# Half the norm matmuls moved to GpSimd adds, a mask in small tiles, ten value moves, full-array norm turns and new step orders in a one-core transformer kernel

## What is computed

```python
for i in range(DEPTH):                                    # 6 layers, 16 batches each
    x = attn_layer(shift_tokens(x), Wqkv[i], q_scale[i], k_scale[i], Wo[i]) + x
    x = ffn_layer(shift_tokens(x), ln_g[i], ln_b[i], W1[i], b1[i], W2[i], b2[i]) + x

def attn_layer(x, Wqkv, qs, ksc, Wo):
    q, k, v = heads of (x @ Wqkv)
    q, k = l2norm(q) * qs, l2norm(k) * ksc                # per head and token
    q, k = rotary(q) * scale, rotary(k) / scale
    sim = (q . k over this window and the one before) * 8, masked to 32 keys back, none before token 0
    return softmax(sim) @ v @ Wo
```

## Time and profile before

| what | value |
|---|---|
| median of 3 runs | 3445.39 us (3439.58 to 3446.2) |
| the profiled execution, its own time | 3448.65 us |
| its span from first to last instruction | 3446.9 us |
| mean granted clock of TensorE, share of full speed | 0.991 |
| busy share PE / ACT / DVE / POOL | 97% / 78% / 71% / 42% |
| DMA, mean | 122 GB/s |

### The profile page before, as it was taken

One profiled execution on the slowest core, in us unless ns is written; L12 is line 12 of the kernel. 1 busy time (PEld: TensorE's weight loads), 2 busy tenths in 40 slices (PEclk: granted clock), 3 DMA queues, 4 the chain that ended last, 5 costly groups with the idle time before them and its releaser, 6 DMA issues.

```text
span 3446.9 us, 152524 instructions
## 1 busy us (share of the span) xinstructions
PE 3333.7 (97%) x63228; PEld 2469.4 (72%) x63228; DVE 2439.3 (71%) x5141; ACT 2701.8 (78%) x9033; POOL 1445.0 (42%) x1276
## 2 busy tenths in 40 slices
PE   7789999999999999999999999999999999999997
PEld 4457777777777777777777777777777777777775
DVE  5667777777777777777777777777777767777773
ACT  5667887878787787878788787877878787887875
POOL 2244443444444354444444443453434444443441
PEclk9999999999999999999999999999999999999998
DMA  2056655665655666565565655565565656556563
GB/s 73 1 109 132 131 123 126 134 136 115 147 118 125 129 137 132 128 131 123 120 148 117 139 128 128 122 138 127 121 141 120 132 127 133 122 121 136 114 135 75
DMA packets 361274, 421.43 MB, mean 122 GB/s; under 512 B 52291, under 2 KB 265814, under 8 KB 359814
## 3 DMA queue, kind: packets, MB, share of 16 engines
q1 hardware_dynamic: 360582, 411.67, 55.2%
HBM read 19.30 MB, written 2.10 MB: 6 GB/s over the span
## 4 chain that ended last, share of the span: by engine, by line
PE 70%; POOL 18%; issue 4%; DVE 2%; ACT 1%; DMA 0%; SPq 0%; POOLq 0%; DVEq 0%
PE ring_ps L1234 16%; POOL qs L617 13%; PE out_ps L1326 12%; PE out_ps L1336 10%; PE ring_ps L1279 8%; PE small_ps L1245 6%; PE score_ps L1297 4%; PE ring_ps L1308 4%; PE ring_ps L1372 4%; POOL probs L601 3%; DVE prod L993 2%; PE ring_ps L1269 2%; PE out_ps L1350 2%; PE score_ps L1289 1%; PE small_ps L1253 1%
## 5 line engine op out<-in xcount | busy, mean ns | idle before, releaser
L774 ACT ACTIVATE probs<-score_ps,neg_max,rq 128x64 f32<-128x64 f32 x3072 | 1194.7, 420 | 95.7 <-DVE neg_max L1031 94.5
L993 DVE TENSOR_TENSOR prod<-ring_ps,tables 128x512 f32<-128x512 f32 x1536 | 956.9, 680 | 285.6 <-PE ring_ps L1234 257.8
L617 POOL TENSOR_TENSOR ks<-prod 128x1024 f32<-128x1024 f32 x192 | 452.7, 2358 | 852.5 <-DVE prod L993 852.4
L1234 PE MATMUL ring_ps<-xs,wqk 128*128 128x256 f32 x3072 | 768.9, 388 | 15.5 <-issue 10.6
L774 ACT ACTIVATION_READ_ACCUMULATOR probs<-score_ps,neg_max,rq 128x1 f32 x3072 | 677.1, 220 | 0.0
L730 ACT ACTIVATE square<-ring_ps,biases 128x512 f32<-128x512 f32 x768 | 516.9, 687 | 197.2 <-DVE prod L993 196.0
L1234 PEld LDWEIGHTS ring_ps<-xs,wqk 128*128 128x128 f32 x3072 | 571.1, 191 | 104.3 <-issue 17.6
L601 POOL TENSOR_TENSOR probs<-probs,inv_sums 128x512 f32<-128x512 f32 x384 | 401.1, 1045 | 576.0 <-DVE inv_sums L1045 576.0
L617 POOL TENSOR_TENSOR qs<-prod 128x1024 f32<-128x1024 f32 x192 | 453.4, 2361 | 395.4 <-DVE prod L993 395.4
L1326 PEld LDWEIGHTS out_ps<-pt,v 64*64 64x64 f32 x24576 | 397.0, 135 | 113.5 <-issue 111.6
L763 ACT ACTIVATE att_t<-out_ps 128x512 f32<-128x512 f32 x384 | 217.0, 591 | 297.3 <-PE out_ps L1326 297.2
(11 more groups left out here) (182 smaller groups left out, 3835.6 us busy)
## 6 DMA issues: line engine op xcount, KB each, us to landing
v<-vs SPq DMA_DIRECT2D x1344, 128.0 KB
qt<-qs SPq DMA_DIRECT2D x768, 128.0 KB
kt<-ks SPq DMA_DIRECT2D x768, 128.0 KB
v<-vs SPq DMA_DIRECT2D x192, 64.0 KB
wqk<-in_L_ffn_Wqkv SPq DMA_DIRECT2D x6, 1024.0 KB, 5.1
wv<-in_L_ffn_Wqkv SPq DMA_DIRECT2D x6, 512.0 KB, 5.8
wo<-in_L_ffn_Wo SPq DMA_DIRECT2D x6, 512.0 KB
out_dram<-ks SPq DMA_DIRECT2D x16, 128.0 KB, 1.9
```

The lines of the kernel that those rows point to most:

```text
L617: pool.tensor_tensor(dst, prod_a[p % 2], prod_b[p % 2], ALU.add).then_inc(rot_ready, 1)
L774: last = nc.scalar.activation(probs[i][:, j, e, :], score_ps[e][:, KEYS * j:KEYS * (j + 1)], ACT.Exp, bias=neg_max[:, h:h + 1], scale=rq[p ...
L993: last = V.tensor_tensor((prod_b if a else prod_a)[p % 2][:, f, :] .rearrange("p (u c) -> p u c", u=2), bank[:, :].rearrange("p (u c) -> p ...
L1234: last = mm(bank_of(s)[:, TOKENS * f:TOKENS * (f + 1)], wqk[:, n, 2 * c + f, a, :], xs[:, WINDOW:PADDED], start=True, stop=True)
```

## The change

It touches one mechanism in each of five places and writes all orders anew.

1. **Sums of squares.** A new POOL step AS adds `square[couple][1]` to `square[couple][0]`, once per couple (4 per batch-layer). NK and NQ then run 4 matmuls in place of 8 and wait for the adds instead of for the squares.
2. **Mask.** The two full-array matmuls per query tile become eight of 64 rows by 32 columns, each over 512 columns, in the tile shape of the scores. The constants shrink to one mask per 64 rows and a selector.
3. **Norm turns.** `rk_bf`, `rkt` and `head_sel_bf` are padded with zeros to 128, so TU and KN use the full array.
4. **Value moves.** 10 DMAs per batch-layer in place of 16, with the same bytes; six of them span 64 partitions.
5. **`pt`** gets a buffer for each query tile, so TC waits for the PV of the previous batch-layer and not for that of the previous tile.

```diff
-V_MOVES = 16
+V_MOVES = 10
 PE_ORDER = """
-PA0 PB0 PA1 S00 S01 PB1 BI WO PA2 NK CEN PB2 VAR PA3 PB3 TK UP0 UP1 S10 S11 V0 UP2 T00 TU NQ KN0 PAD V1 PV00 KN1
-TQ T01 V2 DN T10 PV01 V3 T11 PV10 PV11
+PA0 PB0 S00 S01 BI PAD PB1 PA1 WO PA2 NK PB2 CEN PB3 VAR PA3 TK S10 S11 UP0 UP1 T00 UP2 TU V1 KN0 PV00 KN1 NQ
+T01 V3 DN PV01 T10 TQ V0 V2 T11 PV10 PV11
 DVE_ORDER = """
-XS RA0 RB0 RA1 M0 RB1 BI XA XB AR00 RA2 RB2 CK XG RB3 RA3 H0 M1 AR01 H1 TC00 UC H2 KM0 CQ VC1 KM1 AR10 TC01 X
-AR11 TC10 VC3 TC11
+XS RA0 RB0 BI M0 RB1 RA1 XA RA2 XB AR00 RB2 CK RB3 RA3 XG M1 H0 TC00 AR01 UC H1 H2 KM0 VC1 KM1 AR10 TC01 CQ VC3
+X AR11 TC10 TC11
 ACT_ORDER = """
-QA0 QB0 QA1 E00 QB1 E01 E02 SQ QA2 LN E03 QB2 RTK LG G0 QB3 QA3 G1 VC0 G2 LE E10 E11 E12 E13 VC2 OC00 OC01 OC10
-RTQ OC11
+QA0 QB0 E00 QB1 QA1 E01 E02 QA2 SQ E03 LN RTK QB2 LG G0 QB3 QA3 G1 G2 LE E10 E11 E12 E13 OC00 OC01 RTQ VC0 VC2
+OC10 OC11
 POOL_ORDER = """
-AD0 AD1 AD2 AN00 AD3 RK TB0 AN01 TB1 AN10 TB2 AN11 TB3
+AD0 AS0 AS1 AD1 AN00 AD2 AD3 RK AS2 TB0 TB1 TB2 AN01 AS3 AN10 TB3 AN11
...
+                    top, low = KEYS * e, KEYS * e + WINDOW
+                    for m in range(WPT - 1):
+                        sp.dma_start(v2[top:top + KEYS, m + 1::WPT, :], vs[WINDOW * m:WINDOW * m + KEYS, :, e, :]
+                                     ).then_inc(v_moved, 16)
+                    sp.dma_start(v2[low:low + WINDOW, 0::WPT, :], vs[0:WINDOW, :, e, :]).then_inc(v_moved, 16)
+                    sp.dma_start(v2[top:top + WINDOW, WPT, :], vs[P - WINDOW:P, 0, e, :]).then_inc(v_moved, 16)
...
+                if kind == "AS":
+                    p = s[1]
+                    last_square = max(rank(ACT_ORDER, (x, p), "QA", "QB") for x in ("QA", "QB"))
+                    pool.wait_ge(sq_ready, at(g, QK_BANKS, last_square + 1))
+                    one, other = square[p % COUPLES]
+                    pool.tensor_tensor(one[:, :], one[:, :], other[:, :], ALU.add).then_inc(sq_summed, 1)
...
-                    dve.wait_ge(pv_ready, at(g, TILES, i))
-                    V.tensor_copy(pt[:, 4 * c:4 * c + 4, :], bank_of(("T", i, c))[:, :].rearrange("p (j c) -> p j c", c=P)
+                    if g > 0:
+                        dve.wait_ge(pv_ready, at(g - 1, TILES, i + 1))
+                    V.tensor_copy(pt[i][:, 4 * c:4 * c + 4, :], bank_of(("T", i, c))[:, :].rearrange("p (j c) -> p j c", c=P)
...
-                    pe.wait_ge(sq_ready, at(g, QK_BANKS, last_square + 1))
+                    pe.wait_ge(sq_summed, at(g, 2 * COUPLES, COUPLES * (n + 1)))
                     pe.wait_ge(norms_ready, at(g, 2, n))
-                    for a in range(2):
-                        for u in range(QUADS):
-                            last = mm(norm2_ps[WINDOW * u:WINDOW * (u + 1), :], head_ones[:, :],
-                                      square[u // 2][a][:, TOKENS * (u % 2):TOKENS * (u % 2 + 1)],
-                                      start=(a == 0), stop=(a == 1), skip_group_check=True)
+                    for u in range(QUADS):
+                        last = mm(norm2_ps[WINDOW * u:WINDOW * (u + 1), :], head_ones[:, :],
+                                  square[u // 2][0][:, TOKENS * (u % 2):TOKENS * (u % 2 + 1)],
+                                  start=True, stop=True, skip_group_check=True)
...
-                    turn = bank_of(s)[0:3 * HEADS, 0:TOKENS // 2].bitcast(BF16)
+                    turn = bank_of(s)[:, 0:TOKENS // 2].bitcast(BF16)
...
-                        for e in range(2):
-                            if e == 1 and i == 0:
-                                pe.wait_ge(q_moved, moved(g, 1))
-                            mm(score_ps[e][:, :], ident_bf[:, :], mask_bf[:, i, :, :].rearrange("p j c -> p (j c)"),
-                               start=True, stop=False, skip_group_check=True)
+                        for w in range(WPT):
+                            for e in range(2):
+                                if (w, e) == (WPT - 1, 1) and i == 0:
+                                    pe.wait_ge(q_moved, moved(g, 1))
+                                mm(score_ps[e][WINDOW * w:WINDOW * (w + 1), :],
+                                   mask_sel_bf[64 * e:64 * e + 64, int((i, w) == (0, 0)), :],
+                                   mask_bf[64 * e:64 * e + 64, :, :].rearrange("p j c -> p (j c)"),
+                                   start=True, stop=False, skip_group_check=True)
```

More of the change, by code:

```diff
@@ L32 @@
 MOVES = 8
-V_MOVES = 16
+RK_PARTS = P // HEADS
+V_MOVES = 10
 V_STEPS = 2 * TILES
@@ L138, in build @@
         ident_bf = sb("ident_bf", [P, P], BF16)
-        mask_bf = sb("mask_bf", [P, TILES, PAIRS, KEYS], BF16)
+        mask_bf = sb("mask_bf", [P, PAIRS, KEYS], BF16)
+        mask_sel_bf = sb("mask_sel_bf", [P, 2, WINDOW], BF16)
         head_ones = sb("head_ones", [P, WINDOW])
-        head_sel_bf = sb("head_sel_bf", [3 * HEADS, QUADS, P], BF16)
+        head_sel_bf = sb("head_sel_bf", [P, QUADS, P], BF16)
         rotary = sb("rotary", [P, 2, 2, TOKENS])
@@ L187, in build @@
         inv_sums = [sb(f"inv_sums{i}", [P, PAIRS, 2]) for i in range(TILES)]
-        pt = sb("pt", [P, PAIRS, P])
+        pt = [sb(f"pt{i}", [P, PAIRS, P]) for i in range(TILES)]
         att_t = sb("att_t", [P, PAIRS, TOKENS])
@@ L280, in build @@
         mod_a = carve(P, BATCH, 6)
-        mask = carve(P, TILES, KEYS)
-        head_sel = carve(3 * HEADS, QUADS, P)
+        mask = carve(P, KEYS)
+        mask_sel = carve(P, 2, WINDOW)
+        head_sel = carve(P, QUADS, P)
         wmod = carve(P, 6 * DIM)
@@ L310, in build @@
             sem("f_" + n) for n in ("qkv sq eps inv q2 k2 v kcol max kmax log r qfin kv kvt qt qtc kw kg y gw xb x1").split())
-        xs_ready, proj_ready, prod_ready, sq_ready, rot_ready, v_made, v_even_ready, v_odd_ready = (
-            sem(n) for n in ("xs_ready", "proj_ready", "prod_ready", "sq_ready", "rot_ready", "v_made",
+        xs_ready, proj_ready, prod_ready, sq_ready, sq_summed, rot_ready, v_made, v_even_ready, v_odd_ready = (
+            sem(n) for n in ("xs_ready", "proj_ready", "prod_ready", "sq_ready", "sq_summed", "rot_ready", "v_made",
                              "v_even_ready", "v_odd_ready"))
@@ L439, in _ @@
             load_x(2)
-            for dst, src in ((mask[:, :, :], t["mask"]), (head_ones[:, :], t["head_ones"]),
+            for dst, src in ((mask[:, :], t["mask"]), (mask_sel[:, :, :], t["mask_sel"]), (head_ones[:, :], t["head_ones"]),
                              (head_sel[:, :, :], t["head_sel"]), (rotary[:, :, :], t["rotary"])):
@@ L552, in _ @@
             pool.tensor_copy(head_sel_bf[:, :, :], head_sel[:, :, :])
-            for i in range(TILES):
-                for j in range(PAIRS):
-                    last = pool.tensor_copy(mask_bf[:, i, j, :], mask[:, i, :])
+            pool.tensor_copy(mask_sel_bf[:, :, :], mask_sel[:, :, :])
+            for j in range(PAIRS):
+                last = pool.tensor_copy(mask_bf[:, j, :], mask[:, :])
             last.then_inc(consts_ready, 1)
@@ L1401, in shape_constants @@
     rotary = np.stack([f.T for f in four], 1).astype(np.float32).reshape(P, 2, 2, TOKENS)
-    query = np.arange(P)[:, None] % WINDOW
+    query = np.arange(WINDOW)[:, None]
     key = np.arange(KEYS)[None, :]
-    hidden = (key > query + WINDOW) | (query > key)
-    mask = np.zeros((P, TILES, KEYS), np.float32)
-    for i in range(TILES):
-        no_window = (i == 0) & (np.arange(P)[:, None] < WINDOW) & (key < WINDOW)
-        mask[:, i] = np.where(hidden | no_window, MASKED, 0.0)
+    mask = np.zeros((2, 64, KEYS), np.float32)
+    mask[:, 0:WINDOW] = np.where((key > query + WINDOW) | (query > key), MASKED, 0.0)
+    mask[:, WINDOW] = np.where(key < WINDOW, MASKED, 0.0)
+    mask_sel = np.zeros((2, 64, 2, WINDOW), np.float32)
+    mask_sel[:, 0:WINDOW] = np.eye(WINDOW, dtype=np.float32)[:, None, :]
+    mask_sel[:, WINDOW, 1] = 1.0
     head_ones = np.zeros((P, WINDOW), np.float32)
-    head_sel = np.zeros((HEADS, QUADS, P), np.float32)
+    head_sel = np.zeros((RK_PARTS, HEADS, QUADS, P), np.float32)
     for r in range(4):
@@ L1413, in shape_constants @@
         for u in range(QUADS):
-            head_sel[4 * u + r, u, HALF * r:HALF * (r + 1)] = 1.0
-    return {"ident": np.eye(P, dtype=np.float32), "mask": mask, "head_ones": head_ones,
-            "head_sel": np.concatenate([head_sel] * 3), "rotary": rotary,
+            head_sel[0:3, 4 * u + r, u, HALF * r:HALF * (r + 1)] = 1.0
+    return {"ident": np.eye(P, dtype=np.float32), "mask": mask.reshape(P, KEYS), "mask_sel": mask_sel.reshape(P, 2, WINDOW), "head_ones": head_ones,
+            "head_sel": head_sel.reshape(P, QUADS, P), "rotary": rotary,
             "biases": np.tile(np.array([LN_EPS, 0.0], np.float32), (P, 1)),
```

17 lines of the change are left out of this document (8 added, 9 removed).

## The result

| | before | after |
|---|---|---|
| median | 3444.7 us (4 runs, 3439.58 to 3446.2) | 3489.55 us (4 runs, 3480.02 to 3494.31) |
| ratio, 95% interval | | 1.0129 (1.0103 to 1.0155) |
| span of the profiled execution | 3446.9 us | 3492.5 us |
| mean granted clock of TensorE | 0.991 | 0.982 |
| typical period | 32.98 us | 32.83 us |

The forecast was 3400, faster.

The account below looks back on a forecast made before the run. PE's own work was taken as the bound. Period gains of -75 us, +21 for table waits and +9 for clock falls made -45, 3448.65 to 3404, forecast as 3400 since the median lies 3.3 below the profiled execution; range 3325 to 3442.

Parts of the forecast that it names:

- What bounds the kernel, and what PE loses: PE's own work is the bound; norm sums, mask and turns save 1.66 us per period, giving 31.45 for PE alone.
- WO's end: In the walk through one period, PE's step WO ends 8.9 us after PA0.
- From NQ to the period's end: PE's last stretch of a period, T01 to the end plus NQ, TQ and V0: 9.5 us.
- What then comes up: POOL's adds and the order behind WO cost PE about 1.1 us before NQ; 0.8 per period remains gained.
- AS1 at 9.7. No stall, with 0.2 to spare: POOL's add before NK ends 9.7 us into the period; NK, due at 9.9, does not wait.
- the walk's 32.3: Period in us found by stepping through the new engine lists from PA0 at 0.
- The walk's wait in front of NQ: PE loses about 1.1 us between UP0 and NQ, as NQ may start at 22.8 instead of 21.7.
- Once per layer: Table steps ahead of AN01 delay NQ by 4.2 us in five periods: +21, and +9 for the lowered clock.
- What costs nothing: Ten value moves are issued and landed in time; MK, TC10 and the smaller constants add no wait either.
- The sum: Total of the terms: -75 + 21 + 9 = -45 us, 3448.65 becoming 3404.
- Rivals: Other outcomes: PE stays the bound (0.22), little comes through (0.14), slower by the clock or by serial mask tiles (0.12 together).
- Slower, by the clock: Waits before NQ regularly lower PE's clock, 1.7 us per fall: 3480 us; chance 0.12 shared with serial tiles.

Follow-up runs that it names:

- e1: Changed kernel with the row maxima kept in PSUM, so neg_max reads one SBUF input instead of two; 3423.53 us, ratio 0.9925.
- e7: Kernel before with 10 value moves in place of 16 and nothing else; 3466.23 us, ratio 1.0046.
- e4: Changed kernel with the 16 value moves of the kernel before; 3466.56 us, ratio 1.0050 to the kernel before.
- e11: e5 with the full-array mask of the kernel before; 3383.94 us, ratio 0.9808 to the kernel before.
- e6: Kernel before with the small-tile masks and full-array norm turns alone, old orders, sums, moves and pt; 3421.39 us, ratio 0.9910.
- e5: Changed kernel with row maxima in PSUM, table steps behind AS3 and 16 value moves together; 3377.27 us, ratio 0.9781 to the kernel before.
- e8: Kernel before with GpSimd's adds and halved norm sums alone, NQ, TQ and CQ placed later; 3534.07 us, ratio 1.0236.
- e9: e5 with NQ moved behind T01 and V3 on PE; 3406.41 us, ratio 0.9876 to the kernel before.
- e2: Changed kernel with AD0 on GpSimd held back until the first query tile's neg_max is done; 3472.04 us, ratio 1.0060 to the kernel before.

## Why the prediction was wrong, point by point

- **What bounds the kernel, and what PE loses**: right in kind, short in sum. Norm sums 0.57 (forecast 0.57), mask 0.22 (0.25), WO's end 8.90 (8.9). From NQ to the period's end 9.34 (from 1615.52 to 1624.86; forecast 9.5). But the turns gave 0.08 of the 0.3 forecast, and PE without its two waits needs 31.71 (32.84 - 0.75 - 0.38), not 31.45. The stretch of the earlier trace rows also holds 93 distances and not 94: the mean period before was 33.52, not 33.16, and the 0.4 by which it exceeds the period taken apart, longer periods with gaps, stayed outside the reading.
- **What then comes up**: the step that failed is "AS1 at 9.7. No stall, with 0.2 to spare". The distance from mask to QB1 was carried over from the earlier trace rows, where `neg_max` took 0.18, into a place where AD0 runs beside it. It took 1.05. AS1 came 8.66 after the mask instead of 7.8, NK waited 0.75, everything behind it moved by that, and the period became 32.84 instead of 32.3. With that one cause taken away (e1) AS1 comes at 7.79 and the typical period is 32.02, below the walk's 32.3. The walk's wait in front of NQ was there, but only 0.48 in e1 where 1.1 was forecast from UP0 to NQ: the steps that PE did not save were taken out of it.
- **Once per layer**: right in kind. Forecast +30, measured +35 in the five periods. The wait was 4.46 where it is 0.38 elsewhere, 20.4 for all five (forecast 21), and the half clock behind it was there; issue gaps that fall into these periods are the rest.
- **What costs nothing**: wrong for the value moves. Their issue and landing are indeed covered, but ten moves add 21 to 24 us of issue waits on PE, and in time 16 us alone (e7) and 23 in the kernel after (e4). The sum had put them at nothing. The small masks add about 20 us of issue waits more (e11), which the sum didn't hold either; with the turns, in the old orders, they gave 29 us of the 70 expected (e6). In these waits PE lacks instructions; how the moves and the masks make them late stays open.
- **Rivals**: "Slower, by the clock" named falls behind waits in front of NQ. The mean clock fell from 0.991 to 0.982, so some 64 us more passed at half clock ((0.018 x 3492 - 0.009 x 3447) x 2), half of which at most is lost. But in the steady part of after 10 of the 15 falls come with issue gaps and 5 with the table gaps, and the typical period holds none. e1, with a mean clock of 0.981, is 66 us faster. It was a part and not the cause. None of the rivals had a VectorE instruction held up by GpSimd. With it the forecast would have been 3400 + 0.75 x 94 = 3470, still 20 short; the value moves (23 in e4) are of that size. e5, which takes out the hold-up of `neg_max`, the table order and the ten moves, is at 3377, 23 below the forecast.

## What to carry to other kernels

Before work moves to GpSimd, list the VectorE instructions whose inputs both lie in SBUF and look at which GpSimd instruction runs beside each in the new order: even one on 16 columns can wait for the end of an add (1.05 instead of 0.18 us here), and its place in the chain sets the price. A duration taken from a trace holds only beside the neighbours that it had there; when an order changes, look at what now runs beside each short instruction. Rare steps in an order list (tables once per layer) are to be walked in their own period, and a step moved away from a wait that it covered is to be charged with that wait (e8, e9).

## What the runs showed of the hardware that was not expected

- VectorE's `neg_max` on 128x16 with two SBUF inputs ended 0.03 to 0.04 us after the GpSimd add beside it, in three kernels (177 cases in after, 92 in e2, 90 in e8); with one input in PSUM it took 174 to 176 ns beside the same add (e1). GpSimd's add kept its 2.35 us throughout. With no add beside it, two SBUF inputs took 0.17 us (e2).
- PE's gaps that the profile puts to no other engine grew with larger DMAs of the same total bytes (21.4 to 42.4 us, e7) and with 12 more small matmuls a period (24.2 to 45.3, e11 against e5). 626 of the 629 such gaps in the fourteen traces end 1.0 to 2.0 us behind the end of a 16 KB packet of the instruction queue q8.
- Eight mask matmuls of 64x32 over 512 bf16 columns took 0.22 us together, where two full-array ones over 512 columns took 0.52 before: they ran side by side.
